# Start-up loads and waits, the order of VectorE's last attention steps, and 127-row transfers: one core, windowed attention with a feed-forward block

## The reference, cut to what matters

```python
qkv = x @ w_qkv                                   # 128 -> 3 * 1024
q, k, v = heads of qkv;  q = q * 64 ** -0.5
sim  = einsum('bhnid,bhnjd->bhnij', q_window, concat(k_bos, k_window))
attn = softmax(where(later, -max, sim))
attn = einsum('gh,bhnij->bgnij', w_th, attn)      # heads are mixed
out  = einsum('bhnij,bhnjd->bhnid', attn, concat(v_bos, v_window))
out  = concat(v at position 0, out) @ w_out + b_out
x = layernorm(x + out)
h = gelu(x / rms(x) @ ternary(w_up).T);  x = layernorm(x + h / rms(h) @ ternary(w_down).T)
```

## Time and profile before

| | us |
|---|---|
| median of 3 runs | 251.7 (251.66 to 251.91) |
| the profiled execution | 252.29 |
| its span, first to last instruction | 250.5 |
| TensorE busy | 228.0, 91% of the span |
| VectorE busy | 176.0, 70% |
| ScalarE busy | 162.9, 65% |
| GpSimd busy | 92.8, 37% |
| DMA, mean rate | 47 GB/s |

### The profile page before, as it was taken

How to read it: one execution, slowest core, us unless ns; L and a number is a source line. 1 busy time by engine, 2 the same in 40 slices (tenths; PEclk the granted TensorE clock), 3 DMA queues, 4 the chain that set the end, 5 groups by cost and what they waited for, 6 DMA issues and landing times.

```text
span 250.5 us, 9873 instructions
## 1 busy us (share of the span) xinstructions
PE 228.0 (91%) x4279; PEld 203.9 (81%) x4279; DVE 176.0 (70%) x461; ACT 162.9 (65%) x311; POOL 92.8 (37%) x111
## 2 busy tenths in 40 slices
PE   7798999999999999999999999999999878999930
PEld 6697989988899998889988788888888757889820
DVE  0643589988677883688467875678567988885870
ACT  2584466777666558974797559755977344988660
POOL 7044114531343351635435251525452622121550
PEclk9999799999999999999999999999999999999975
DMA  6637570020010002000201020010101001000011
GB/s 213 214 90 198 169 199 5 3 65 3 3 55 13 24 3 59 10 25 5 63 4 33 14 64 5 0 47 25 41 3 47 0 3 40 9 1 21 5 44 42
DMA packets 18911, 11.69 MB, mean 47 GB/s; under 512 B 2036, under 2 KB 17972, under 8 KB 18740
## 3 DMA queue, kind: packets, MB, share of 16 engines
...
...
## 4 chain that ended last, share of the span: by engine, by line
PE 53%; DVE 19%; ACT 18%; issue 3%; DMA 2%; POOL 1%; POOLq 0%; SPq 0%; DVEq 0%; ACTq 0%
PE bank L1078 9%; PE bank L1080 8%; PE bank L1079 8%; PE bank L1227 6%; PE bank L1201 6%; DVE CTl L856 5%; ACT CTh L561 3%; PE bank L1185 3%; DVE AT L861 3%; ACT L653 3%; DVE E L870 2%; DMA xq<-in_L_attn_x 2%; ACT Yb L561 2%; ACT gT L653 2%; ACT E L705 2%
## 5 line engine op out<-in xcount | busy, mean ns | idle before, releaser
L856 DVE TENSOR_TENSOR CTl<-bank,CTh 128x512 fp32r<-128x512 f32 x64 | 41.0, 682 | 24.6 <-ACT CTh L561 24.4
L503 POOL TENSOR_TENSOR E<-E,rc 128x400 f32<-128x400 f32 x32 | 27.9, 871 | 81.6 <-DVE rc L878 81.5
L561 ACT ACTIVATE Yb<-bank 128x512 f32<-128x512 f32 x64 | 38.4, 600 | 28.4 <-PE bank L1080 28.0
L1078 PE MATMUL bank<-xTh,Gh 128*128 128x256 f32 x128 | 40.3, 315 | 3.0 <-ACT Yb L561 2.1
L705 ACT ACTIVATE E<-E 128x400 f32<-128x400 f32 x32 | 17.3, 540 | 37.2 <-DVE E L870 37.0
L1078 PE MATMUL bank<-CTh,Mh 128*128 128x256 f32 x128 | 37.0, 289 | 1.9 <-DVE CTl L856 1.9
L1079 PE MATMUL bank<-xTl,Gh 128*128 128x256 f32 x128 | 36.2, 282 | 0.0
L1080 PE MATMUL bank<-CTh,Ml 128*128 128x256 f32 x128 | 36.1, 282 | 0.0
L1080 PE MATMUL bank<-xTh,Gl 128*128 128x256 f32 x128 | 36.0, 281 | 0.0
L1079 PE MATMUL bank<-CTl,Mh 128*128 128x256 f32 x128 | 36.0, 281 | 0.0
L561 ACT ACTIVATE CTh<-bank 128x512 fp32r<-128x512 f32 x64 | 34.7, 599 | 1.9 <-PE bank L1227 1.8
...
## 6 DMA issues: line engine op xcount, KB each, us to landing
...
xr<-in_L_attn_x SPq DMA_DIRECT2D x6, 128.0 KB
out<-y SPq DMA_DIRECT2D x6, 128.0 KB, 1.9
...
```

Source lines behind the costliest of these rows:

```text
L503: tt(e, e, rc[s % 2][:, :].unsqueeze(2).broadcast_to([P, TILES, WIN]), ALU.mult).then_inc(s_norm, 1)
L561: copy = lambda o, i, **k: nc.scalar.activation(o, i, ACT.Copy, **k)
L856: v.tensor_tensor(ct_view(CTl[s // 4 % 2], s % 4, q), c_view(s, q), ct_view(f32(CTh[s // 4 % 2][:, :, :]), s % 4, q), ALU.subtract).then_i ...
L1078: mm(o, wh, rh, start=start, stop=False, **k)
```

## The change

What it does, engine by engine:

- SyncE loads the value weights, behind the second half of the key weights; ScalarE no longer does. Every transfer of 127 rows becomes one of 112 and one of 15 rows (`xq`, `xr`, the stores). `w_ff` is issued ahead of the first window. `PT` is written in two halves, each waiting for its own two `p` fills. The last store of position 0 goes to ScalarE's queue, and the wait for it leaves SyncE.
- The first eight Y blocks take pairs of heads from one `g` fill: block 0 heads 0 and 2, block 1 heads 4 and 6, block 2 heads 1 and 3, and so on, and each pair of blocks waits for its own `g` fill. ScalarE copies them to every second head of `Yb`.
- In step 0 the second Y block goes to bank 3 and waits for one copy less.
- `v0` and `bos` use 32 matmuls of 32 columns of weights each in place of 16 of 64.
- VectorE, steps 28 to 31: `hidden_sum(3)` moves ahead of `shift(28)`, and `second_sum(3)`, `second_norm(3)`, `residual(5)`, and `input_scale(5)` with `up_input(5)`, move between `shift` and `total` of steps 28, 29, 30 and 31.

The diff, cut to its core (the split of `xr` and of the stores of chunks 3 and 7 is of the same kind as that of `xq`; line numbers of the changed kernel differ from those of the profile):

```diff
@@ -263,7 +263,7 @@
...
-            return 3 if n % 4 == 3 else 1
+            return 4 if n % 4 == 3 else 1
@@ -312,6 +312,9 @@
...
+        def y_bank(s, b):
+            return Y_BANK[b if s == 0 else 0]
@@ -321,6 +324,15 @@
...
+        def pair(b):
...
+            return heads(b // 2)[2 * (b % 2):2 * (b % 2) + 2]
...
+        def Y_first(b):
...
+            a, c = pair(b)
+            return Yb[0][:, :, :].rearrange("p t (h i) -> p h t i", i=IL)[:, a:c + 1:2]
@@ -353,8 +365,10 @@
                 sp.dma_start(xq[:, t0:t0 + TPI, :], x[b, 1:1 + ITER_TOK, :].rearrange("(m p) c -> p m c", p=P)).then_inc(s_xq[2 * b], 16)
                 if b == 0:
                     wk_load(1)
+                    sp.dma_start(w_sb[2][:, :], w_qkv[:, 2 * INNER:3 * INNER]).then_inc(s_wv, 16)
                 sp.dma_start(xq[:, t0 + TPI:t0 + 7, :], x[b, 1 + ITER_TOK:897, :].rearrange("(m p) c -> p m c", p=P)).then_inc(s_xq[2 * b + 1], 16)
-                sp.dma_start(xq[0:127, t0 + 7, :], x[b, 897:1024, :]).then_inc(s_xq[2 * b + 1], 16)
+                sp.dma_start(xq[0:112, t0 + 7, :], x[b, 897:1009, :]).then_inc(s_xq[2 * b + 1], 16)
+                sp.dma_start(xq[112:127, t0 + 7, :], x[b, 1009:1024, :]).then_inc(s_xq[2 * b + 1], 16)
 
             x_load(0)
             sp.dma_start(wo_sb[:, :, :], w_out.rearrange("(t p) n -> p t n", p=P)).then_inc(s_wout, 16)
@@ -384,19 +398,21 @@
                         sp.dma_start(raw[row:row + SEG + 1:SEG, :, :],
                                      x[b, 0, :].unsqueeze(0).unsqueeze(1).broadcast_to([2, CPAIR, P])).then_inc(s_raw, 16)
 
+            for i in range(2):
+                sp.dma_start(w_ff[:, i, :].rearrange("p (t d) -> p t d", t=FT) if i == 0 else w_ff[:, 1, :],
+                             w_up.rearrange("(t p) d -> p t d", p=P) if i == 0 else w_down).then_inc(s_wff, 16)
             sp.wait_ge(s_zero, 1)
             sp.wait_ge(s_raw0, 1)
             window(0, 0)
             x_load(1)
-            for i in range(2):
-                sp.dma_start(w_ff[:, i, :].rearrange("p (t d) -> p t d", t=FT) if i == 0 else w_ff[:, 1, :],
-                             w_up.rearrange("(t p) d -> p t d", p=P) if i == 0 else w_down).then_inc(s_wff, 16)
             sp.dma_start(wth8[:, :], w_th.unsqueeze(1).broadcast_to([H, IL, H])).then_inc(s_small, 16)
             sp.dma_start(b_sb[:, :], b_out.rearrange("(c o) -> c o", o=1)).then_inc(s_small, 16)
-            sp.wait_ge(s_eva, read_no("A", "p", 2))
-            sp.wait_ge(s_evd, read_no("D", "p", 3))
-            sp.dma_start(pt_rows.rearrange("g o c -> o g c"), PT[:, :, :]).then_inc(s_pt, 16)
-            sp.wait_ge(s_pt, 16)
+            for half in range(2):
+                sp.wait_ge(s_eva, read_no("A", "p", 2 * half))
+                sp.wait_ge(s_evd, read_no("D", "p", 2 * half + 1))
+                hs = slice(8 * half, 8 * half + 8)
+                sp.dma_start(pt_rows[hs].rearrange("g o c -> o g c"), PT[:, hs, :]).then_inc(s_pt, 16)
+            sp.wait_ge(s_pt, 32)
             sp.dma_start(R[:, :, :], pt_rows.rearrange("g (a b) c -> (g a) b c", a=IL)).then_inc(s_R, 16)
             flat = out.rearrange("b n c -> (b n) c")
 
@@ -410,7 +426,8 @@
...
-                    sp.dma_start(xr[n == 7][0:P - 1, 1, :], x[b, t0 + P:N, :]).then_inc(s_xr[n == 7], 16)
+                    sp.dma_start(xr[n == 7][0:112, 1, :], x[b, t0 + P:t0 + P + 112, :]).then_inc(s_xr[n == 7], 16)
+                    sp.dma_start(xr[n == 7][112:P - 1, 1, :], x[b, t0 + P + 112:N, :]).then_inc(s_xr[n == 7], 16)
@@ -442,8 +460,6 @@
...
-            sp.wait_ge(f_out7, 2)
-            sp.dma_start(flat[B * N - N:B * N - N + 1, :], y2[own(n)][P - 1:P, 1, :]).then_inc(f_store[own(n)], 16)
@@ -564,7 +580,6 @@
...
-            act.dma_start(w_sb[2][:, :], w_qkv[:, 2 * INNER:3 * INNER]).then_inc(s_wv, 16)
@@ -595,7 +610,7 @@
...
-                copy(Y_out(b, 0, 2 * b), bank[Y_BANK[b % 2]][:, :].rearrange("p (h t i) -> p h t i", h=2, i=IL)).then_inc(s_Ye, 1)
+                copy(Y_first(b), bank[Y_BANK[b % 2]][:, :].rearrange("p (h t i) -> p h t i", h=2, i=IL)).then_inc(s_Ye, 1)
@@ -623,7 +638,7 @@
...
-                         bank[Y_BANK[0]][:, :].rearrange("p (h t i) -> p h t i", h=2, i=IL)).then_inc(s_Ye, 1)
+                         bank[y_bank(s, b)][:, :].rearrange("p (h t i) -> p h t i", h=2, i=IL)).then_inc(s_Ye, 1)
@@ -770,7 +785,10 @@
...
-            act.dma_start(flat[B * N - P + 1:B * N, :], y2[own(7)][0:P - 1, 1, :]).then_inc(f_store[own(7)], 16)
+            t0 = B * N - P + 1
+            act.dma_start(flat[t0:t0 + 112, :], y2[own(7)][0:112, 1, :]).then_inc(f_store[own(7)], 16)
+            act.dma_start(flat[t0 + 112:B * N, :], y2[own(7)][112:P - 1, 1, :]).then_inc(f_store[own(7)], 16)
+            act.dma_start(flat[B * N - N:B * N - N + 1, :], y2[own(7)][P - 1:P, 1, :]).then_inc(f_store[own(7)], 16)
@@ -984,19 +1002,31 @@
                     if k == 2:
                         x1_lo(n)
                 if s == LAG + 1:
-                    dve.wait_ge(s_pt, 16)
+                    dve.wait_ge(s_pt, 32)
                 if s > LAG:
                     ct_lo(s - LAG - 1)
                 if s >= LAG:
                     at_lo(s - LAG)
+                for n, k in ffn(s):
+                    if k == 5 and n == 3:
+                        hidden_sum(n)
                 for n, k in ffn(s):
                     if k == 1:
                         input_scale(n)
                         up_input(n)
                 shift(s)
                 for n, k in ffn(s):
-                    if k == 5:
+                    if k == 5 and n < 3:
                         hidden_sum(n)
+                    if k == 5 and n == 3:
+                        second_sum(n)
+                    if k == 6 and n == 3:
+                        second_norm(n)
+                    if k == 0 and n == 5:
+                        residual(n)
+                if s == STEPS - 1:
+                    input_scale(5)
+                    up_input(5)
                 if s < 2:
                     absolute_sum(s)
                 if s == 2:
@@ -1023,16 +1053,14 @@
                 if s == 6:
                     fills(IN_STEP[6][-1:])
                 for n, k in ffn(s):
-                    if k == 0:
+                    if k == 0 and n < 5:
                         residual(n)
-                    if k == 6:
+                    if k == 6 and n < 3:
                         second_norm(n)
 
             at_lo(30)
             ct_lo(29)
-            input_scale(5)
             at_lo(31)
-            up_input(5)
             ct_lo(30)
             ct_lo(31)
             x1_lo(5)
@@ -1079,10 +1107,10 @@
...
-            def y_part(bk, chunk_cols, h0):
...
-                for n in range(2):
-                    ins = split3(bank[bk][:, CHUNK * n:CHUNK * (n + 1)], Gh[:, h0 + n, :], Gl[:, h0 + n, :],
+            def y_part(bk, chunk_cols, hs):
...
+                for n, h in enumerate(hs):
+                    ins = split3(bank[bk][:, CHUNK * n:CHUNK * (n + 1)], Gh[:, h, :], Gl[:, h, :],
@@ -1094,7 +1122,7 @@
...
-                        pe.wait_ge(s_xq[i], 48 if i % 2 else 16)
+                        pe.wait_ge(s_xq[i], 64 if i % 2 else 16)
@@ -1142,15 +1170,15 @@
...
-                            for lo in (0, 64):
+                            for lo in range(0, P, 32):
...
-                                ins = mm(bnk[lo:lo + 64, 2 * k:2 * k + 2], w_sb[2][:, c:c + 64], x0T[:, :],
+                                ins = mm(bnk[lo:lo + 32, 2 * k:2 * k + 2], w_sb[2][:, c:c + 32], x0T[:, :],
...
-                            for lo in (0, 64):
-                                ins = mm(bnk[lo:lo + 64, 0:2], wo_sb[:, k, lo:lo + 64], v0T[:, 2 * k:2 * k + 2],
+                            for lo in range(0, P, 32):
+                                ins = mm(bnk[lo:lo + 32, 0:2], wo_sb[:, k, lo:lo + 32], v0T[:, 2 * k:2 * k + 2],
@@ -1160,12 +1188,12 @@
             fills(FILLS)
 
             for b in range(8):
-                if b % 4 == 0:
-                    pe.wait_ge(s_eva, read_no("A", "g", 1 + b // 2))
-                    pe.wait_ge(s_evd, read_no("D", "g", 1 + b // 2))
+                if b % 2 == 0:
+                    pe.wait_ge(s_eva, read_no("A", "g", b // 2))
+                    pe.wait_ge(s_evd, read_no("D", "g", b // 2))
                 if b >= 2:
                     pe.wait_ge(s_Ye, b - 1)
-                y_part(Y_BANK[b % 2], slice(0, CHUNK), 2 * b)
+                y_part(Y_BANK[b % 2], slice(0, CHUNK), pair(b))
                 if b % 2 == 1:
                     fills(BETWEEN[b // 2])
             pe.wait_ge(s_evd, read_no("D", "x", 1))
@@ -1307,9 +1335,9 @@
             def queries(s, b):
 
                 if s < STEPS - 4:
-                    pe.wait_ge(s_Ye, 8 + 2 * s + b)
+                    pe.wait_ge(s_Ye, 8 + 2 * s + b - (s == 0))
                     c = (s // 4 + 1) % 6
```

(3 more changed lines are left out.)

5 lines of the change are left out of this document (3 added, 2 removed).

## The result

| | before | after |
|---|---|---|
| median, the same chip (us) | 251.81 | 245.05 (244.70 to 245.56) |
| ratio, 95% interval | | 0.973 [0.971, 0.976] |
| the same on another chip | 252.48 | 245.14, 0.972 [0.969, 0.976] |
| profiled execution, its span | 252.29, 250.5 | 244.73, 242.9 |

6.8 us faster (7.3 on the other chip), 245.0 was forecast. The sum is right, its terms are not: the start brought less than I counted, the last steps and the store more.

A forecast was written before the change was run, and what follows sets the result against it. Bounds: TensorE at the start, VectorE in steps 28 to 31, the last store's transfer. Savings 3.3 + 1.6 + 1.8 = 6.7 us take the profiled 252.29 to 245.6; less 0.6 for the median, 245.0 us, range 243.3 to 247.5.

The forecast's parts named there:

- First Y block, 0.65; second one of step 0, 0.69: Start: waiting for the first `Gl` alone saves 0.65 us; bank 3 removes the second block's 0.69 us wait.
- `v0` and `bos`, 0.56: Start: 64 passes of 32 columns take 0.75 us instead of 1.03, saving 0.28 each, 0.56 for both.
- Rival 4: `v0` and `bos`: each pass keeps its 32 ns spacing, 1.31 us more than counted, twice: 247.6 us; chance 0.03.
- The clock, 1.38: Behind `v0`, TensorE runs at half clock and loses 1.38 us; all of it was counted as regained.
- Start 3.3, loads 0 ("just fits"): Start terms sum to 3.3 us (1.9 to 3.6); second window's rows just keep up, cost 0, up to 1.5.
- VectorE's last steps, 1.6: Steps 28 to 31: pieces moved into VectorE's 0.6 us waits for the exponential save 1.6 us, 2.1 at best.
- Rival 3: Last steps: ScalarE's splits or TensorE's output products set the pace, only 0.6 of 1.6 comes: 246.0 us; chance 0.13.
- The last store, 1.8: End: 127 rows ride one DMA engine for 3.0 us; splitting the store saves 1.8 us, at the outside 1.2 to 2.4.
- rival 6: Last store: 112 rows are no better spread than 127, its 1.8 us is lost: 246.8 us; chance 0.03.
- Rivals 1: Start: the clock falls all the same, here or at another pause, price 1.4 us: 246.4 us; chance 0.18.
- 2: Step 4: the second window binds, TensorE waits at the transposes, price 0.8 us: 245.8 us; chance 0.12.
- 5: Loads: SyncE's queue clogs, `PT` and `R` go out 5.16 us later: 252.8 us; chance 0.04.

The follow-up runs named there:

- the order alone: The kernel before with only VectorE's new order in steps 28 to 31 changed: 250.64 us, ratio 0.992 [0.988, 0.995].

## Why the prediction was right, and where its terms were wrong

*First Y block, 0.65; second one of step 0, 0.69.* Right in place and size (0.85 and no idle time left; over all profiles the first block starts at 11.0 to 11.8 with the old wait and at 10.6 to 11.3 with the new one, 0.6 apart in the mean).

*`v0` and `bos`, 0.56.* 0.27 and about as much: the size is right, the worth is not. They only bring TensorE to its next cap; with wide blocks the kernel is as fast. Rival 4 (a price by the piece) is out: 64 passes in 0.76 us.

*The clock, 1.38.* The failing step. I took a stretch of one execution for a property of the kernel, and counted its removal against a median that holds executions with and without it. The same start ran at full clock in another profile. The size was right for the execution that I read: from step 0's maximum to step 12's it took 65.39 us, and 64.02 at full clock, 1.37 less. What the change does is to take away the condition under which it fell four times of five. The Trainium skill could have warned me ("TensorE: Matmul & The Clock Gate", section "Part 1: The HAM clock gate"): it says of the slow stretch at the start of a kernel that its extent differs between runs of the same kernel. The traces show the like for a stretch some 25 us into one.

*Start 3.3, loads 0 ("just fits").* Read at step 2 against the dented start it is 3.60, against a full-clock start 2.50, and 1.1 to 1.4 are left at step 12. "It just fits" was wrong by at least 1.1: I had looked for one cap in steps 3 and 4, the window. There are three within 1 us of each other: TensorE's instruction packets, the window's rows, and VectorE. The window was in fact binding at full clock before the change (0.47 us of waiting in the profile of the order alone), and in the changed kernel it isn't the one that is last.

*VectorE's last steps, 1.6.* The mechanism held, 2.50 came. The 0.6 of idle time per step were right. 0.15 to 0.38 more each came on top. In part it is from small operations that ran right behind the sum beside GpSimd's normalisation and now don't, and from one piece that left step 28; what the rest of it is, no run isolates. Two rows show the first kind, VectorE in step 28 before and after:

```profile
197.66 0.33 DVE L951 SCALAR_TENSOR_TENSOR floor<-hden 128x2 f32<-128x2 f32 x1
```

```profile
193.94 0.15 DVE L969 SCALAR_TENSOR_TENSOR floor<-hden 128x2 f32<-128x2 f32 x1
```

The 0.2 that I took off for step 31 was not due: 6.48 before and after. Rival 3 (hand-over) is out.

*The last store, 1.8.* Worth 3.0, beyond my outer end of 2.4. I took 1.9 us from issue to landing from transfers of 128 KB; the last issue ends at 241.52 and the span at 242.9, so the 64 KB and less of the end are in within 1.4 us of it, the span's own end included, and by the last two stretches above they had moved by about 242.0, 0.5 behind the issue. The step that failed is this one time to landing. The split is right (0.80 of the DMA engines' time against 0.07): rival 6 is out.

*The sum.* Measured against full clock 1.4 + 2.5 + 3.0 = 6.9, of which 0.3 is lost in between (0.12 up to step 28, 0.19 behind the last product), and a median of 6.8; mine 3.3 + 1.6 + 1.8 = 6.7. The errors are -1.9, +0.9 and +1.2: the time came out by cancelling, and the forecast is no proof of its working. There was luck in the step to the median too. From profiled execution to profiled execution the gain is 252.29 - 244.73 = 7.56, since the first of them had the dent, and I had forecast 245.6 for it, 0.9 too much; the 0.6 that I took off to get from the profile to the median hid most of that, though the profiled execution of the changed kernel lies 0.3 below its median and not 0.6 above. Rivals 1, 2 and 5 didn't come about, though what 2 describes (a transfer keeps its own time, TensorE sits in front of it) did, with another transfer.
